# Cross-attention of 16 heads: the next head's squared queries turned ahead of P, and their row sums taken behind P's normalization

## The reference, cut to what matters

```python
def rmsnorm(x, g, eps=1e-5):
    var = jnp.mean(jnp.square(x), axis=-1, keepdims=True)
    return x * jax.lax.rsqrt(var + eps) * g
...
q = (hidden_states @ Wq).reshape(B, Sq, H, D)
k = (encoder_hidden_states @ Wk).reshape(B, Skv, H, D)
v = (encoder_hidden_states @ Wv).reshape(B, Skv, H, D)
q = rmsnorm(q, gq)
k = rmsnorm(k, gk)
scores = jnp.einsum('bqhd,bkhd->bhqk', q, k) * scale
attn = jax.nn.softmax(scores, axis=-1)
out = jnp.einsum('bhqk,bkhd->bqhd', attn, v)
out = out.reshape(B, Sq, H * D)
return out @ Wo
...
x = x + jnp.tanh(g_xattn[3]) * _L3_xattn_ref(_layernorm(x, axis=-1), ctx_1024, ...)
```

## Time and profile before

| what | value |
|---|---|
| median of three executions | 3784.42 us |
| the profiled execution, its own time | 3780.23 us |
| its span, first to last instruction | 3778.6 us |
| TensorE busy | 3554.1 us, 94% |
| TensorE weight loads busy | 1932.9 us, 51% |
| VectorE busy | 3001.6 us, 79% |
| ScalarE busy | 1751.4 us, 46% |
| GpSimd busy | 649.4 us, 17% |
| mean granted TensorE clock | 0.973 |
| the chain of work that ended last | PE 56%, DVE 22%, issue 11%, ACT 7%, DMA 3% |

### The profile page before, as it was taken

The page is one execution under the profiler, slowest core; times in us unless marked ns, Lnnn a source line. Parts: engine busy times, 40 slices in busy tenths (PEclk is TensorE's granted clock), DMA queues, the critical chain, the costliest instruction groups (busy, mean ns, idle before and its releaser), DMA issues.

```text
span 3778.6 us, 39496 instructions
## 1 busy us (share of the span) xinstructions
PE 3554.1 (94%) x11937; PEld 1932.9 (51%) x11954; DVE 3001.6 (79%) x4927; ACT 1751.4 (46%) x2739; POOL 649.4 (17%) x596
## 2 busy tenths in 40 slices
PE   8999999899999998899999999999999999999787
PEld 4656565544444444444446788554454454454343
DVE  7898988797979787889989777685585585686597
ACT  5868777633332323334444211463353353353376
POOL 1424252243434110234421000000000000000000
PEclk8999999999999999999999999999999999999898
DMA  3324241524233312444345201221121121121000
GB/s 134 123 74 144 66 148 54 195 87 166 92 134 124 125 65 86 167 156 139 108 150 209 78 25 48 98 74 45 41 72 45 44 69 45 44 69 60 1 12 34
DMA packets 90982, 344.78 MB, mean 91 GB/s; under 512 B 11808, under 2 KB 20128, under 8 KB 77504
## 3 DMA queue, kind: packets, MB, share of 16 engines
q1 hardware_dynamic: 61264, 225.86, 16.9%
q0 software_dynamic: 29552, 116.94, 9.2%
HBM read 280.36 MB, written 62.39 MB: 91 GB/s over the span
## 4 chain that ended last, share of the span: by engine, by line
PE 56%; DVE 22%; issue 11%; ACT 7%; DMA 3%; POOL 0%; DVEq 0%; ACTq 0%; POOLq 0%; SPq 0%
PE ps L1171 35%; PE ps L1559 6%; PE ps L1390 3%; PE ps L1257 3%; PE ps L1549 3%; DVE room L1722 2%; PE ps L1442 2%; DVE room L1726 2%; DVE room L1730 1%; DMA room<-bc_scratch 1%; PE ps L1244 1%; DVE stat L1686 1%; DVE room L1735 1%; DMA kv_stash<-room 1%; PE ps L1529 1%
## 5 line engine op out<-in xcount | busy, mean ns | idle before, releaser
L1171 PE MATMUL ps<-lnT,room 128*128 128x512 f32 x2240 | 990.7, 598 | 19.4 <-DVE room L1931 11.4
L1171 PE MATMUL ps<-room 128*128 128x512 f32 (+2 forms) x1871 | 714.9, 537 | 50.4 <-DVE xres L2218 17.9
L1171 PEld LDWEIGHTS ps<-lnT,room 128*128 128x128 f32 x2240 | 428.0, 192 | 566.1 <-issue 534.0
L659 POOL TENSOR_TENSOR idle<-idle 128x1 f32<-128x1 f32 x268 | 474.7, 1771 | 1252.1 <-ACT room L844 434.6
L1171 PEld LDWEIGHTS ps<-room 128*128 128x128 f32 (+1 forms) x1888 | 309.8, 168 | 432.7 <-issue 318.2
L1390 PE MATMUL ps<-room 128*128 128x512 f32 x864 | 376.2, 593 | 7.4 <-DVE room L1883 7.4
L771 ACT ACTIVATE room<-room,small 128x511 f32<-128x511 f32 x256 | 163.6, 710 | 361.8 <-DVE room L1726 361.7
L1780 DVE TENSOR_TENSOR_SCAN room<-room 128x2048 f32<-128x2048 f32 x64 | 283.2, 4425 | 16.3 <-ACT room L834 10.9
L1726 DVE TENSOR_TENSOR_SCAN room<-room 128x2048 f32<-128x2048 f32 x64 | 283.4, 4427 | 5.4
L1390 PEld LDWEIGHTS ps<-room 128*128 128x128 f32 x864 | 163.6, 190 | 212.2 <-issue 206.4
L1074 ACT ACTIVATE room<-ps,stat 128x512 f32<-128x512 f32 x256 | 199.0, 777 | 136.2 <-DVE stat L2179 136.2
(11 more groups left out here) (237 smaller groups left out, 5053.0 us busy)
## 6 DMA issues: line engine op xcount, KB each, us to landing
room<-in_ffn SPq DMA_DIRECT2D x16, 2048.0 KB, 10.7
room<-bc_scratch POOLq DMA_DIRECT2D x128, 256.0 KB, 3.6
room<-kv_stash SPq DMA_DIRECT2D x64, 512.0 KB, 3.5
kv_stash<-room POOLq DMA_DIRECT2D x96, 256.0 KB, 2.4
room<-stash POOLq DMA_DIRECT2D x24, 1024.0 KB, 5.2
room<-in_ffn SPq DMA_DIRECT2D x20, 1024.0 KB, 5.7
room<-in_ffn SPq DMA_DIRECT2D x24, 768.0 KB, 5.7
room<-in_ffn SPq DMA_DIRECT2D x12, 1536.0 KB, 8.2
```

What stands on the lines that cost most here:

```text
L659: nc.gpsimd.tensor_tensor(idle[:, :], idle[:, :], idle[:, :], ALU.add).then_inc(zeros_added, 1)
L1171: last = nc.tensor.matmul(out, lhsT, rhs, start=(i == 0), stop=(i == len(parts) - 1))
```

## The change

TensorE turns the squares of head h + 1 in place of head h + 2, and does it ahead of the turn of P in place of behind it. VectorE takes their sums behind P's normalization, right ahead of `normalize`, in place of at the start of the head. So the squares of head 1 no longer have to be turned ahead of the loop over heads, and this call goes at the batch turn and ahead of the first batch. The helpers `query_sums` and `take_sums` themselves stay as they are, their waits too.

```diff
--- before
+++ after
@@ -1542,14 +1542,14 @@
                             product(ps[:, 4 + t, :], [(h_q[h % 2][:, t * P:(t + 1) * P], h_kT[h % 2])]).then_inc(h_s, 1)
                         if h + 2 < H:
                             queries(b, h + 2)
+                        if h + 1 < H:
+                            query_sums(b, h + 1)
                         for k in range(NT):
                             for t in range(NT):
                                 if k == 0:
                                     pe.wait_ge(h_P_ready, (b * H + h) * NT + (t + 1))
                                 mm = nc.tensor.transpose(ps[:, 4 + k, t * P:(t + 1) * P], P3[:, t, k * P:(k + 1) * P], ident[:, :])
                             mm.then_inc(h_tr, 1)
-                        if h + 2 < H:
-                            query_sums(b, h + 2)
                         kv = t3(h_kv[h % 2], NT)
                         pe.wait_ge(h_out_ready, b * H + h)
                         for k in range(NT):
@@ -1572,7 +1572,6 @@
                         query_sums(b + 1, 0)
                     project(b, 2)
                     if not last:
-                        query_sums(b + 1, 1)
                         keys_transposed(b + 1, 0)
                     project(b, 3)
 
@@ -1584,7 +1583,6 @@
                 product(ps[:, 0, 0:B], [(ones[:, :], stat[:, 120:120 + B])]).then_inc(b_sum, 1)
                 queries(0, 1)
                 query_sums(0, 0)
-                query_sums(0, 1)
                 keys_transposed(0, 0)
                 pe.wait_ge(b_sum, 2)
                 batches(pe, body)
@@ -2171,8 +2169,6 @@
 
                 def body(b, last):
                     for h in range(H):
-                        if h + 1 < H:
-                            take_sums(b, h + 1)
                         for t in range(NT):
                             dve.wait_ge(h_s, (b * H + h) * NT + (t + 1))
                             link(v.tensor_reduce(mx[:, t:t + 1], ps[:, 4 + t, :], AX.X, ALU.max, negate=True))
@@ -2182,6 +2178,7 @@
                             link(v.reciprocal(inv[:, t:t + 1], total[:, t:t + 1]))
                             v.tensor_scalar(P3[:, t, :], P3[:, t, :], inv[:, t:t + 1], None, ALU.mult).then_inc(h_P_ready, 1)
                         if h + 1 < H:
+                            take_sums(b, h + 1)
                             normalize(b, h + 1)
                         round_bit(b, h)
                     def add(t):
```

## The result

The changed kernel took 3871.51 us in the median of four executions (3868.29 to 3875.00), the kernel before 3785.58 beside it. The ratio is 1.0231, with a 95% interval of 1.0215 to 1.0247: **slower by 2.3%**, 85.9 us.

A forecast was written before the change was run, and what follows sets the result against it. TensorE (13.11 us a head) was taken as bound, VectorE's loop (13.04) close behind and pacing after the change. Terms 85.0 + 3.2 + 0.7 - 1.3 = +87.6 us gave a forecast of 3872, range 3850 to 3900.

The forecast's parts named there:

- The bound: Steady head before the change: TensorE needs 13.11 us, VectorE's loop through the keys 13.04, with 0.07 to spare.
- (a): Sum of squares moves on VectorE to between P and normalization: 1.03 us a head in batches 1 to 3, 0.93 in the last.
- (b): Sum waits for the same head's turn of squares: starts at 7.61, 0.70 us later than VectorE could.
- (c): On TensorE the turn of squares (0.43 us) goes ahead of P's turn; P times V still starts at 9.15.
- Heads 1 to 13: Steady heads of four batches: 1.66 us more a head, 1.56 in the last batch, together 85.0.
- Heads 0 and 14: Head 0: +3.2 us from first and last batch, zero in the others; head 14: +0.7 in sum.
- Batch turns: One turn of squares less among the projections at each of three batch turns: -1.3 us.
- The sum: Whole kernel: +87.6 us in all, a forecast median of 3872.0.
- The first: Rival: on VectorE only the moved instructions count, not the wait for squares; 14.07 us a head, 3834; chance 0.06.
- The third: Rival: VectorE's 0.89 us of idle time takes up the sum, TensorE stays the bound; 3783; chance 0.05.
- The second: Rival: TensorE's granted clock falls in the new gaps, in half of 54 heads +44 us, 3916; chance 0.07.

The follow-up runs named there:

- VectorE's part alone: Kernel before with only the sums moved right ahead of normalize, TensorE turning squares two heads ahead and behind P as before: 3833.14 us, ratio 1.0124.

## Why the prediction was right, point by point

- *The bound.* The order of time gave 13.11 for TensorE and 13.04 for VectorE's loop. Both were later seen by themselves: 13.11 with a shorter loop, 13.03 with less of TensorE's work.
- *(a), the moved instructions.* Forecast 1.03 in the loop over batches and 0.93 in the last batch. In the loop it is 0.93 and 1.01 in turn from head to head, so the term was over-sized by 0.06 there. Alone it cost 48.
- *(b), the wait.* Forecast a sum at 7.61, 0.70 later than VectorE could; it starts at 7.61, behind 0.61 of idle time as the row shows it, and heads differ by 0.69 with and without it. Alone it is worth 37.
- *(c), TensorE's order.* P times V starts at 9.15 before and after. Moving the squares once more, ahead of the queries, left the heads as with VectorE's part alone: the order costs nothing but the wait.
- *Heads 1 to 13.* 85.0 forecast, 82.7 measured. The larger part of the 2.3, 1.5 us, is that I set 13.11 for heads that took 13.15 on average in the three looped batches. The rest is 0.02 a head (14.75 for 14.77): (a) was over-sized by 0.06 there, and three of the thirteen heads, at 14.83 to 15.09, give the larger part of that back.
- *Heads 0 and 14.* In head 0 of the second batch, whose scores start at 2707.32, the first maximum came after 2.24 us (3.48 before) and the sum after 7.88, behind no idle time, where I had 8.08:

```profile
2709.56 0.69 DVE L2174 TENSOR_REDUCE stat<-ps 128x1 f32<-128x512 f32 x1 [2.29 <-PE ps L1171]
...
2715.20 0.68 DVE L2134 TENSOR_REDUCE stat<-ps 128x4 f32<-128x512 f32 x1
```

  The head takes 15.02 where it took 15.24, in the third batch 15.20 where it took 15.13; I had said no change. Head 14, from first maximum to first maximum, took 14.2, 14.0, 14.0 and 14.2 against 15.2, 13.8, 14.0 and 13.5: in sum -0.2 against my +0.7. The three that I had forecast gave +0.8; the first, which I had left at nothing, gave back 1.1, as its granted clock rose from 0.78 to 0.88.
- *Batch turns.* -1.3 forecast, -3.6 measured; but in two of them the first maximum, which ends my stretch, comes 2.2 us earlier in sum and is paid for inside the heads. Without that it is -1.4, and heads 0 are +3.1 against my +3.2.
- *The sum.* +87.6 forecast, +85.9 between medians. The profiled executions are 88.1 apart, but 3.9 of that lies outside the stage; its own +84.2 is the number to hold against 87.6. That the forecast median of 3872.0 came within 0.5 us is luck: the stage's own difference is 3.4 short of the forecast, and what lies outside the stage, with the spread between executions, happened to make up for it.
- *Rivals.* The first fell: the instructions alone are 3833, where I had 3834, and the whole is 38 more. The third fell: VectorE's idle time is real at the old place (a second sum is free) and does not help at the new one. The second did not happen here but was not far off: with 0.6 us more of waiting the clock fell in some heads. The rows before could not tell 1.4 from 1.57 us of waiting, so the chance of 0.07 was a guess, and the clock's holding was not derived.

## What to carry to other kernels

Idle time has a place: before moving an instruction into an engine's spare time, walk the loop once around and see whether that time lies ahead of or behind the result that another engine waits for. Here 0.9 us of idle time stood behind the keys and was worth nothing to an instruction ahead of them. When a producer's step is moved closer to its consumer, set both on one clock: the squares could not be turned before 7.57, and the consumer was there at 6.91. Where two engines need nearly the same time, shortening either alone gains little and the pair pays: thirteen heads of the first batch gained 0.5 us by VectorE's shorter loop, 0.8 by TensorE's shorter turn, and 3.0 by both. And a busy share of 100% does not show which engine sets the pace: TensorE had it at 13.03 us a head, bound by VectorE, and at 12.92.

## What the runs showed of the hardware

- TensorE's granted clock stayed at 1.00 (2.4 GHz) through 52 heads with a wait of 1.32 to 1.60 us each. With waits of 1.92 us and more it fell to 0.50 (1.2 GHz) in 16 of 52 heads and not in the others, at 1.5 us a fall; after one and the same wait of 1.93 us it did either. Twelve 128-column turns put into that wait, work that is thrown away, kept it at 1.00 and made the kernel 33 us faster.
- Two row sums that follow each other without a semaphore between them start 0.60 us apart, though each is shown with 0.68.
- Four bfloat16 products of 128 x 128 with one column take 0.18 us from start to the next start, the four float32 turns 0.43.
